# Own buffer for projection squares, shifts issued by GpSimd, loads in pieces, a new order of all engines, and four slots for first-layer weights

## The reference

```python
xn = layernorm(x)
q, k, v = split(xn @ W_qkv.T + b_qkv)           # 8 heads of 16 channels
q, k, v = (t / norm(t) * exp(1j * phase) for t in (q, k, v))   # per head
for depth in range(3):                          # q and k only
    s1, s2 = state[..., :-1, :], state[..., 1:, :]        # neighbouring heads
    new = |s1|**2 * rot(s2) + (1 - |s1|**2) * s2          # head h controls head h+1
    state = concat(new, last head)
for c in range(4):                              # circuits, per token, heads x heads
    scores = |conj(qa) @ ka|**2 / 4
    w = sqrt(softmax(scores) + 1e-12)
    co = (w @ v) * coherence phase              # clipped to 1e-6..1 in magnitude
    final += sup_w[c] * co
attention = real(final) @ W_out.T + b_out
# experts: 8 of them, 128 -> 512 -> 128, the two best per token
cw = softmax of the two best of xn @ Wg
experts = sum_e cw[e] * (gelu(xn @ W1[e] + b1[e]) @ W2[e] + b2[e])
```

## Time and profile before

| | before |
|---|---|
| median of the runs shown | 1360.44 us (1360.26 to 1366.40) |
| the profiled execution, its own time | 1359.84 us |
| its span, first to last instruction | 1358.1 us |
| mean granted TensorE clock | 0.784 |
| PE, DVE, ACT, POOL busy | 63%, 52%, 54%, 32% |
| DMA | 143.33 MB, 106 GB/s on average |

### The profile page before, as it was taken

How to read it: one execution, slowest core, us unless ns; L and a number is a source line. 1 busy time by engine, 2 the same in 40 slices (tenths; PEclk the granted TensorE clock), 3 DMA queues, 4 the chain that set the end, 5 groups by cost and what they waited for, 6 DMA issues and landing times.

```text
span 1358.1 us, 28230 instructions
## 1 busy us (share of the span) xinstructions
PE 852.2 (63%) x10145; PEld 709.2 (52%) x10145; DVE 702.7 (52%) x1278; ACT 730.7 (54%) x1586; POOL 432.9 (32%) x389
## 2 busy tenths in 40 slices
PE   3412785864762867678564876777376677777531
PEld 2301774754651756657454665667365575657420
DVE  6572454755462463657344565666244544764340
ACT  3422674744462665666453766667276665675231
POOL 4055100016052040504617050323834140533164
PEclk9955887887886888887786978787687887877755
DMA  8127165573837238484383746465293847475822
GB/s 259 78 64 151 39 112 91 110 104 79 136 88 114 52 86 140 86 137 77 108 119 85 143 84 103 89 129 106 81 157 89 139 84 131 94 123 104 144 54 50
DMA packets 300713, 143.33 MB, mean 106 GB/s; under 512 B 151651, under 2 KB 278307, under 8 KB 300067
## 3 DMA queue, kind: packets, MB, share of 16 engines
q1 hardware_dynamic: 278051, 95.36, 41.5%
q10 hardware_dynamic: 14336, 29.37, 8.1%
q0 software_dynamic: 8192, 16.79, 4.8%
HBM read 65.28 MB, written 57.28 MB: 90 GB/s over the span
## 4 chain that ended last, share of the span: by engine, by line
issue 25%; POOL 18%; DMA 16%; DVE 11%; PE 10%; SPq 9%; ACT 8%; ACTq 1%; DVEq 1%; POOLq 0%
POOL rows_in L1258 9%; DMA sqy<-sqx 5%; DMA xn<-in_L_attn_query_dram 4%; DVE xy L1444 4%; POOL got L1274 3%; PE ps_h L646 3%; POOL sqx L1230 3%; SPq L533 3%; SPq L534 2%; DMA x_tile<-rows_in 2%; ACT hid L1067 2%; PE ps_k L719 2%; DVE xy L1624 2%; DMA states<-sqy 1%; DMA k_rows<-states 1%
## 5 line engine op out<-in xcount | busy, mean ns | idle before, releaser
L1230 POOL TENSOR_TENSOR sqx<-sqx,sqy 128x512 f32<-128x512 f32 x64 | 88.7, 1407 | 635.0 <-ACT sqy L979 634.7
L646 PE MATMUL ps_h<-turned,w_up 128*128 128x128 f32 x1248 | 213.6, 324 | 110.9 <-ACT turned L1060 105.4
L646 PEld LDWEIGHTS ps_h<-turned,w_up 128*128 128x128 f32 x1248 | 186.8, 228 | 147.5 <-ACT turned L1060 130.4
L1067 ACT ACTIVATE hid<-ps_h,w_up 128x128 f32<-128x128 f32 x624 | 177.8, 371 | 72.8 <-PE ps_h L646 49.0
L661 PE MATMUL ps_f<-w_res,hid 128*128 x1248 | 198.1, 310 | 7.7 <-issue 4.3
L661 PEld LDWEIGHTS ps_f<-w_res,hid 128*128 128x128 f32 x1248 | 181.4, 223 | 15.9 <-issue 13.2
L1258 POOL DMA_INDIRECT rows_in<-xn,row_of x128 | 135.8, 1061 | 64.6 <-issue 36.6
L719 PE MATMUL ps_k<-w_proj,xnT 128*128 128x384 f32 x128 | 78.6, 707 | 111.5 <-ACT xy L950 111.1
L1698 DVE COPY w_up<-w_res 128x516 f32 x156 | 82.7, 535 | 122.5 <-ACT hid L1067 103.9
L1274 POOL DMA_INDIRECT got<-rows_out,row_of x112 | 117.4, 1048 | 88.4 <-DMA rows_out<-turned 54.5
L731 PE MATMUL ps_a<-k_rows,q_rows 128*32 128x16 f32 x4096 | 101.2, 248 | 64.1 <-DMA k_rows<-states 59.8
(11 more groups left out here) (247 smaller groups left out, 1525.0 us busy)
## 6 DMA issues: line engine op xcount, KB each, us to landing
states<-xy ACTq DMA_DIRECT2D x32, 512.0 KB
k_rows<-states SPq DMA_DIRECT2D x128, 128.0 KB, 6.7
x_tile<-rows_in SPq DMA_DIRECT2D x156, 64.0 KB
rows_out<-turned SPq DMA_DIRECT2D x156, 64.0 KB
q_rows<-states SPq DMA_DIRECT2D x128, 64.0 KB, 6.2
sqy<-sqx SPq DMA_DIRECT2D x16, 448.0 KB, 3.7
sqy<-sqx SPq DMA_DIRECT2D x16, 384.0 KB
rows_in<-v_rows SPq DMA_DIRECT2D x2, 2496.0 KB, 10.3
```

What stands on the lines that cost most here:

```text
L646: last = nc.tensor.matmul(ps_h[:, c, :], w_up[:, n % WS, c * P:(c + 1) * P], turned[:, x_turn(n) % FS, 0, :], start=True, stop=True)
L1067: act.activation(hid[:, n % 2, c, :], ps_h[:, c, :], ACT.Gelu, bias=w_up[:, n % WS, HID + c:HID + c + 1]).then_inc(hidden_ready.sem, 1)
L1230: pool.tensor_tensor(out_, a, b, op).then_inc(sig.sem, 1)
```

## The change

The squares of the projection get a buffer of their own, and `copy_proj` waits for the sums of the block before (`ss_step`) in place of its `d2_ready`. The wait for `d2_ready` moves to `control_states`, which writes `xy2`. `shift_first` and `shift_last` become POOL's and stand right behind the sums that they move. SP's list is rewritten: `load_x` at the head of the step (block 5 already before the steps), `load_states` in four pieces of four DMAs, `load_values` in four of four, `load_mixed` at the end of its own step. POOL's scatters move behind the second sum, and in step -1 also the ones that stood before it. The opening of a group (`open_group`) moves from its slot to the end of the slot before. `WS` goes from 3 to 4; `xnT` from 6 slots to 5, `yacc` from 6 to 5; `par` and `half` move into scratch. The lists of PE, ACT and DVE are written anew. The diff, cut to its core:

```diff
-YS = 6
-WS = 3
+XT_KEPT = 5
+YS = 5
+WS = 4
...
-        sq = xy2.rearrange("p a g c -> p (a g c)")[:, 0:T * QKV].rearrange("p (t c) -> p t c", t=T)
+        sq = sb("sq", [P, T, QKV])
...
             def copy_proj(k, at):
...
-                    act.wait_ge(d2_ready.sem, d2_ready.value(o))
+                    act.wait_ge(ss_step.sem, ss_step.value(o))
...
             def control_states(k):
                 act.wait_ge(sq0_ready.sem, sq0_ready.value(k))
-                act.wait_ge(ss_step.sem, ss_step.value(k))
+                if k >= 1:
+                    act.wait_ge(d2_ready.sem, d2_ready.value(k - 1))
...
+            def shift_first(k):
+                pool.wait_ge(sum1_ready.sem, sum1_ready.value(k))
+                pool.dma_start(sqy[HD:C], sqx[0:NT * HD]).then_inc(first_shifted, 16)
+
+            def shift_last(k):
+                pool.wait_ge(sum2_ready.sem, sum2_ready.value(k))
+                pool.dma_start(sqy[2 * HD:C], sqx[HD:NT * HD]).then_inc(last_shifted, 16)
+                pool.dma_start(sqy[0:HD], sqx[NT * HD:C]).then_inc(last_shifted, 16)
```

POOL's list of one step, before and after:

```diff
                 if exists(n):
                     sum_squares(n, sq1_ready, sum1_ready)
-                scatter_part(k, 0)
-                scatter_part(k, 1)
+                    shift_first(n)
+                if exists(n):
+                    normalise_values(n)
                 for b in combined[0:1]:
                     add_rows(b)
                 for b in combined[1:2]:
                     gather(b)
                 if exists(n):
-                    normalise_values(n)
-                if exists(n):
                     sum_squares(n, sq2_ready, sum2_ready)
+                    shift_last(n)
+                scatter_part(k, 0)
+                scatter_part(k, 1)
+                if len(combined) < 2:
+                    for b in coming:
+                        gather(b)
+                scatter_part(k, 2)
+                scatter_part(k, 3)
...
```

More of the change, by code:

```diff
@@ L244, in build @@
                    expo.rearrange("p c n -> p (c n)")]
+        par, half = scratch[0][:, 1024:1144], scratch[0][:, 1152:1248]
         ang, kk, rem = (scratch[0][:, n * NANG:(n + 1) * NANG] for n in range(3))
@@ L542, in load_mixed, with open_group, tile_rows @@
                     sp.dma_start(meas[32 * s:32 * s + 32].rearrange("p t (i d) -> p (t i) d", d=HD), src[s]).then_inc(mixed_loaded, 16)
+            def open_group(k, at):
+                for n in step_tiles.get(k, [])[at:at + 1]:
+                    if n % TILES == 0:
+                        for m in range(XT):
+                            load_rows(n + m)
+            def tile_rows(k, at):
+                for n in step_tiles.get(k, [])[at:at + 1]:
+                    s = n % TILES
+                    store_tile(n)
+                    if s + XT < TILES:
+                        load_rows(n + XT)
+                open_group(k, at + 1)
             load_first(0)
@@ L579, in _ @@
             for k in STEPS:
+                o, n, j, far = k - 1, k + 1, ln_block(k), k + 2
                 for b in combined_at.get(k - 1, []):
                     store(b)
-                if exists(ln_block(k)):
-                    load_x(ln_block(k))
+                open_group(k, 0)
+                if exists(j) and j >= 6:
+                    load_x(j)
+                if exists(k):
+                    load_values(k, 2)
+                tile_rows(k, 0)
+                if exists(k):
+                    load_values(k, 3)
@@ L584, in _ @@
                 if exists(k):
                     load_base(k)
[L586 to L597, removed]
-                    if at == 8 and exists(n_next):
-                        load_states(n_next)
-                    n = tiles_now[at] if at < len(tiles_now) else None
-                    if n is None:
-                        continue
-                    s = n % TILES
-                    if s == 0:
-                        for m in range(XT):
-                            load_rows(n + m)
-                    store_tile(n)
-                    if s + XT < TILES:
-                        load_rows(n + XT)
+                tile_rows(k, 1)
@@ new lines, in _ @@
+                tile_rows(k, 2)
+                tile_rows(k, 3)
+                tile_rows(k, 4)
+                if exists(n):
+                    store_values(n)
+                tile_rows(k, 5)
+                tile_rows(k, 6)
+                if exists(n):
+                    load_states(n, 0)
+                if exists(n):
+                    load_states(n, 1)
+                if exists(n):
+                    load_states(n, 2)
+                tile_rows(k, 7)
+                if exists(n):
+                    load_states(n, 3)
@@ L610, in _ @@
+                if exists(n):
+                    load_values(n, 0)
+                tile_rows(k, 8)
+                if exists(n):
+                    load_values(n, 1)
+                tile_rows(k, 9)
+                tile_rows(k, 10)
+                if exists(k):
+                    load_mixed(k)
             for b in combined_at.get(NB, []):
@@ L827, in _ @@
                     target_tiles(n)
+                second_layers(k, 0)
+                if routed is not None and k >= 0:
+                    rank_rows(routed)
                 if exists(k):
@@ L881, in _ @@
                     weighted(k, 1, 1)
+                first_layers(k, 8)
+                second_layers(k, 8)
+                if exists(k):
+                    mix_circuits(k)
                 first_layers(k, 9)
@@ L895, in _ @@
             act.wait_ge(setup_psum, 2)
-            act.activation(par[:], ps_k[:, 0:120], ACT.Copy).then_inc(setup_copied, 1)
+            act.activation(par, ps_k[:, 0:120], ACT.Copy).then_inc(setup_copied, 1)
             act.wait_ge(setup_psum, 3)
@@ L1075, in hidden @@
                         gelu(n)
+            def hidden(k, at):
+                for n in step_tiles.get(k, [])[at:at + 1]:
                     if n % TILES + 1 < TILES:
@@ L1124, in _ @@
                     control_states(n)
-                turned_rows(k, 0)
-                if routed is not None:
+                if routed is not None and k >= 0:
                     copy_sums(routed)
@@ L1132, in _ @@
                     pass_first(n)
+                hidden(k, 0)
+                turned_rows(k, 0)
                 if exists(k):
```

244 lines of the change are left out of this document (125 added, 119 removed).

## The result

The changed kernel takes 1194.16 us (median of four runs, 1187.97 to 1198.68) against 1362.39 for the kernel before, run beside it on the same chip: a ratio of 0.8759, 95% interval 0.8704 to 0.8814. Predicted were 1190 us in a range of 1105 to 1325, and faster. The profiled execution is the slowest of the four, 1198.68 us with a span of 1196.9, at a mean granted clock of 0.816 (before: 0.784).

A forecast was written before the change was run, and what follows sets the result against it. No engine was full, so waits between engines were taken to set the span. 134.0 + 4 + 928.5 + 25 + 22 + 75.1 = 1188.6 us, with 1.7 us from span to time 1190 us; range 1105 to 1325.

The forecast's parts named there:

- three parts: Span before the first expert tile (134.0 + 4 us), the fifteen middle steps (928.5 + 25 + 22), and the tail (75.1).
- The openings: Group starts waiting for later scatters: 17 us of stall in step 7, some 5 in step 11, together 22 us.
- the slower rival that priced it by bytes: POOL's shift issues cost by bytes, up to 8.8 us each: 13.8 us a step more, 1411 us; chance 0.10.
- 45 less 22 and 4: Scatters behind the second sum: steps 2, 6, 10 lose 15 us holes; openings cost 22, the first tile 4.
- the 1.7 between 2.4 and 0.7: Shifts issued by POOL: the second comes 2.4 us sooner, the first about 0.7 us later, in each step.
- The loads and stats, 7 to 13 us a step: Loads in pieces on SP and `layer_norm_stats` later on DVE: 7 to 13 us per step on the path.
- the 25 us for the layer norm: Layer norm work in ten steps, missing from the step of 61.9 us: estimated 2.5 us a step, 25 us.
- 61.9: Shortest step shown before the change, 61.9 us, without the two large holes; taken for all fifteen steps: 928.5 us.
- 60 to 66: Sign of being right: windows by step read 60 to 66 us, with PE's granted clock above 0.82.
- my own 68: Sign of being wrong: plain steps over 68 us; DMA shares over 0.75 were another.
- half of the excess stays with DMA (1276): Rival: busier DMA engines stretch landings, so the fifteen steps take 69.3 us each, 1276 us; chance 0.24.
- openings replace the holes in full (1360): Rival: new holes at the head of a step replace those removed, 11 us a step, about 1360 us; chance 0.04.

The follow-up runs named there:

- the split: The changed kernel with the first part of each step's scatters put between the two sums on POOL: 1183.22 us, ratio 0.8695.
- The last experiment: The changed kernel with the first part of the scatters between the two sums and seven `x_tile` buffers for five: 1151.13 us, ratio 0.847.

## Why the prediction was right, point by point

*The sum.* Its three parts came out within 7 us each, but in the middle two errors cancel, and that is luck. The openings cost 39.5 us, not 22, and the rest of the middle 942.7, not 953.5. PE's waits in the changed kernel:

```profile
387.03 0.47 PE L651 MATMUL ps_f<-ident,x_tile 128*128 128x128 f32 x1 [13.35 <-DMA x_tile<-rows_in]
...
644.18 0.48 PE L651 MATMUL ps_f<-ident,x_tile 128*128 128x128 f32 x1 [20.03 <-DMA x_tile<-rows_in]
...
888.10 0.47 PE L651 MATMUL ps_f<-ident,x_tile 128*128 128x128 f32 x1 [6.10 <-DMA x_tile<-rows_in]
```

Steps 7 and 11 were predicted at 17 and 5 by counting POOL's scatters. Step 3 I had at nothing. The kernel before already had these waits, 21.14, 11.83 and 7.75 us in the same three steps; two of its rows, PE's wait for `x_tile` in all and its opening in step 7:

```profile
PE ps_f L638 <- DMA x_tile<-rows_in: 84.7, 8, 21.1
```
```profile
737.29 0.47 PE L638 MATMUL ps_f<-ident,x_tile 128*128 128x128 f32 x1 [11.83 <-DMA x_tile<-rows_in]
```

Together 40.7 us before and 39.5 after: the change moved the openings' waits from step 3 to step 7 and did not add to them, while the sum booked them as a new cost. Step 3's is set by SP's queue, not POOL's:

```profile
373.34 0.32 SPq L521 DMA_DIRECT2D q_rows<-states  x1
...
378.54 0.43 SPq L522 DMA_DIRECT2D k_rows<-states  x1
379.01 0.45 SPq L485 DMA_DIRECT2D rows_out<-turned  x1
379.56 2.27 SPq L481 DMA_DIRECT2D x_tile<-rows_in  x5
```

The issue of the last scatter ends at 373.9; twelve state DMAs go out ahead of the `x_tile` loads of 379.56, and PE has the rows at 387.0. With the scatters done some 9 us earlier, as in the split, this wait is still 13.07 us. I had counted what the openings wait for on POOL and not what stands ahead of them on SP. Where I did count states ahead of an `x_tile`, I put three groups at six DMAs; they are twelve, as these rows show (5.7 us from the first to the tile's store).

*The terms.* POOL's shift issue was sized at 1.26 us and is 0.50 to 0.75; the slower rival that priced it by bytes falls with the same rows, as no issue comes near 6.7 us (its own terms give a threshold of 7.2 us a shift: 10.6 a step, plus the 3.76 already counted, over two shifts). The Trainium skill, SBUF — State Buffer, section "SBUF: two separate sides", would have let a GpSimd issue wait for a VectorE instruction in a two-port mode. The longest of 48 issues is 0.25 us above the shortest, so no such wait is seen in an issue; but it is hardly tested, as no issue had one of the growth's `tensor_scalar` of 0.79 us beside it: the growth waits for the shift. The scatter of 1.95 us in the earlier trace rows had none beside it either, but two `tensor_tensor` on `xy` (630.92 to 633.27) and a reduction, so whether it is a case of that rule stays open. Undoing the scatter's move costs 12 us, against 19 by my terms (45 less 22 and 4): its steps grow by 21 us, not 45. Undoing the shifts' move costs 13, against 27 (16 times the 1.7 between 2.4 and 0.7). The loads and stats, 7 to 13 us a step, cost 127 us undone in part (the value loads stayed in pieces), 8.5 a step.

*Where the reasoning was thin.* I gave the gain to four edits and costed the new order of PE, ACT and DVE at nothing or as fill. The runs show that the edits don't add up: undone one at a time they cost 57, 127, 13 and 12 us, 209 in all, where the whole gain is 169; added to the old orders, squares, stats and POOL's order together bring 45, and SP's order on top of these loses 83. The forecast came out on the mean: the middle less the openings and the 25 us for the layer norm is 61.2 us a step, where I took 61.9. I chose that number from one step of the kernel before; no run shows why the mean should meet it. I did write that `layer_norm_stats` is covered by its later place. I did not see that by putting `load_mixed` ahead of `load_x` the change itself makes the early place worse than before (20.11 us of standing against the 13.01 of the earlier trace rows).

*What should be seen.* DVE's `stats` and ACT's `qkv` waits are gone from the steps; the second sum starts 0.1 us after ACT's squares in fifteen of sixteen blocks (620.38 against 620.31 in step 7) and 6.3 us after them in step 13. The middle makes 65.5 us a step at a clock of 0.85, inside 60 to 66 on the mean only: cut at `control1`, the fourteen steps from 149.9 to 1061.5 run from 52.7 to 80.5 us, and none lies between 60 and 66. Step 7, 75.2 us, is not the longest: step 3 takes 80.5, with the opening that I had at nothing and 58.5 us of PE's work. The plain step of 69.00 us shown above is over my own 68, with a DMA share of 0.81 over my 0.75, and it is not alone: steps 1 and 8 take 70.2 and 68.5 us, steps 8 and 12 have shares of 0.79. By my own signs that is against me. The last experiment shows what it was: with seven buffers steps 1, 5 and 8 take 58.8, 60.9 and 58.8 us (68.5, 68.0 and 68.1 with the split alone), step 5 at a share of 0.83, so the late `x_tile` loads held them and not the engines' share.

*Rivals.* That half of the excess stays with DMA (1276) did not happen, but the mechanism did in part: outside the openings PE waits for `x_tile` in thirteen places, some 44 us in all (113.6 less the 30.4 of the first opening and the 39.5 above), and asking for it earlier was worth 31 us (1183 to 1151). In the slower kernel with the squares back in `xy2` none of the thirteen is left: there another wait covers them. That openings replace the holes in full (1360) did not.

*Left open.* What the orders of PE, ACT and DVE bring one by one, and the fourth weight slot by itself, were not tried; the runs bound them only together: 207 us between the kernel with POOL's and SP's orders (1401) and the changed kernel, the place of `load_mixed` included.

## What to carry to other kernels

When engines' orders are written by hand, an edit is worth what the other orders let it be worth: price it undone in the new kernel and alone in the old, and believe neither by itself. For a wait on a load, compare when the consumer asks with when the issuing queue gets to it and with what stands ahead of it there; the landing time (4 us here, in a wait of 20) is often the small part. A request that depends only on a free buffer should be asked for early enough that requests ahead of it in the queue, which wait for other engines, do not make it late: two more buffers bought 31 us here.

## What was not expected of the hardware

The first shift, a plain DMA of 448 KB in 112 rows, costs POOL's queue 0.55 to 0.75 us to issue and lands in a median of 4.4 us; issued by SP it takes 0.52 to 0.61 and lands in 3.8. POOL pays less for it than for the indirect DMA of 128 rows of 512 B, 0.96 us and a gap of 0.30. And the granted clock before the first tile was 0.74 in the changed kernel's profile and 1.00 in that of the fastest, with PE busy for 41.46 and 41.92 us and the first tile at 137.8 and 138.0 us. From 88 to 104 us the same ten matmuls take 6.00 us at a granted 0.50 and 5.96 at 1.00: in that stretch neither the matmuls nor the span follow the granted clock, and no run shows why.
